# Rows of the right-hand table as one fp32 value or as three bf16 parts, in the edge loop of a graph attention kernel

## The reference

```python
xl = (x @ W_l).reshape(N, HEADS, HEAD_DIM)
xr = (x @ W_r).reshape(N, HEADS, HEAD_DIM)
e = xl[src] + xr[dst]
e = jnp.where(e >= 0, e, NEG_SLOPE * e)
score = jnp.einsum('ehd,hd->eh', e, att)
m = jax.ops.segment_max(score, dst, num_segments=N)
...
ex = jnp.exp(score - m[dst])
denom = jax.ops.segment_sum(ex, dst, num_segments=N)
alpha = ex / (denom[dst] + SM_EPS)
agg = jax.ops.segment_sum(alpha[:, :, None] * xl[src], dst, num_segments=N)
```

## Time and profile before

| | us |
|---|---|
| median of the runs | 1655.17 |
| lowest and highest | 1635.84 and 1659.02 |
| the profiled execution | 1631.12 |
| its span in the profile | 1629.4 |

### The profile page before, as it was taken

The page is one execution under the profiler, slowest core; times in us unless marked ns, Lnnn a source line. Parts: engine busy times, 40 slices in busy tenths (PEclk is TensorE's granted clock), DMA queues, the critical chain, the costliest instruction groups (busy, mean ns, idle before and its releaser), DMA issues. The chain is left out here.

```text
span 1629.4 us, 25059 instructions
## 1 busy us (share of the span) xinstructions
PE 1216.3 (75%) x5659; PEld 863.3 (53%) x5659; DVE 1080.2 (66%) x2307; ACT 846.6 (52%) x3252; POOL 817.7 (50%) x849
## 2 busy tenths in 40 slices
PE   7938677777677777777776768777777756399995
PEld 5426555555455555555554556555555545255663
DVE  7735777677667766776676766786677859313444
ACT  3501366665567557665765676676666813132221
POOL 5454356565456545555555565555656064402223
PEclk9978899989798978999998888999889977599998
DMA  6554357566556655565665666666765125325340
GB/s 184 172 150 114 107 156 172 155 170 163 153 141 169 166 153 143 166 170 157 168 162 138 166 161 167 171 171 166 207 160 137 44 63 178 141 95 151 103 122 17
DMA packets 169375, 238.14 MB, mean 146 GB/s; under 512 B 41666, under 2 KB 135571, under 8 KB 169284
## 3 DMA queue, kind: packets, MB, share of 16 engines
q1 hardware_dynamic: 125188, 130.89, 28.5%
q0 software_dynamic: 41216, 103.67, 24.9%
q10 hardware_dynamic: 2880, 2.66, 0.5%
HBM read 189.57 MB, written 49.58 MB: 147 GB/s over the span
## 5 line engine op out<-in xcount | busy, mean ns | idle before, releaser
L1083 POOL DMA_INDIRECT gathered_rows<-d_xl,e_idx x576 | 547.3, 950 | 420.0 <-ACT e_prod L1512 195.7
L1512 ACT ACTIVATE e_prod<-gathered_rows,e_prod 128x64 f32<-128x64 f32 x2728 | 676.6, 335 | 30.7 <-issue 22.8
L1457 PE MATMUL bank<-e_prod,e_selt 128*128 128x260 f32 x1408 | 409.8, 436 | 157.2 <-DMA gathered_rows<-in_src_dram,n_row_of 68.8
L1457 PEld LDWEIGHTS bank<-e_prod,e_selt 128*128 128x128 f32 x1408 | 286.9, 212 | 250.0 <-issue 89.2
L1403 PE MATMUL bank<-e_xr,e_sel 128*128 128x256 bf16 x2112 | 325.5, 292 | 52.8 <-issue 31.3
L1157 DVE TENSOR_TENSOR e_edge<-bank,gathered_rows 128x512 f32<-128x512 f32 x176 | 119.9, 681 | 285.9 <-remote 271.3
L1403 PEld LDWEIGHTS bank<-e_xr,e_sel 128*128 128x128 bf16 x2112 | 217.6, 105 | 152.6 <-issue 70.1
L1408 PE MATMUL bank<-gathered_rows,ident 128*128 128x256 f32 x704 | 229.4, 406 | 14.0 <-issue 14.0
L1174 DVE TENSOR_REDUCE e_score<-e_edge 128x16 f32<-128x1024 f32 x176 | 213.2, 1211 | 0.3
L1508 ACT ACTIVATE e_prod<-e_diff 128x16 f32<-128x16 f32 x176 | 39.4, 224 | 237.6 <-remote 111.1
L1083 POOL DMA_INDIRECT gathered_rows<-d_xl,src_cols x112 | 106.3, 949 | 105.0 <-issue 29.4
(11 more groups left out here) (315 smaller groups left out, 1105.7 us busy)
## 6 DMA issues: line engine op xcount, KB each, us to landing
e_xr<-d_xr SPq DMA_DIRECT2D x176, 192.0 KB
d_hist<-e_acc SPq DMA_DIRECT2D x176, 130.0 KB
e_drow<-d_rel SPq DMA_DIRECT2D x176, 128.0 KB
w_rows<-in_L_ffn_w_dram SPq DMA_DIRECT2D x16, 1024.0 KB, 7.3
gathered_rows<-d_xl,e_idx POOLq DMA_INDIRECT x576
d_in<-lambda_w SPq DMA_DIRECT2D x18, 387.0 KB
e_rows<-d_rows SPq DMA_DIRECT2D x88, 48.1 KB
x_rows<-in_x_dram SPq DMA_DIRECT2D x8, 512.0 KB, 4.8
```

What stands on the lines that cost most here:

```text
L1083: pool.indirect_dma_start(xl[:, q.slot * G + g, :], None, m.d_xl, bass.IndirectOffsetOnAxis(ap=column, axis=0)).then_inc(gathered[q.slot], 16)
L1457: last = pe.matmul(ps_agg[b], selt[:, b, g, :], flat(prod[:, b, g, :, :]), start=(g == 0), stop=(g == G - 1))
L1512: last = act.activation(prod[:, b, g, h, 0:HEAD], xl[:, q.slot * G + g, h * HEAD:h * HEAD + HEAD], ACT.Copy, scale=prod[:, b, g, h, HEAD:H ...
```

## The change

The right rows are stored once, as fp32. `d_xr` has 256 fp32 columns, a row block is 128 KB, and the survey's steps for the second and third part go (L486, L490, L870); L866 writes the row. The one-hot `sel` becomes fp32. `edges` makes one fp32 one-hot product a group (four a quad in place of twelve), and one fp32 identity product of 512 columns over the adjacent slots of groups 0 and 1 in place of two of 256. The identity product now opens the bank, and the one-hot products of groups 0 and 1 are added to it. The wait for the gathers stands behind groups 2 and 3.

```diff
@@ tensors of the module
-    m.d_xr = dram("d_xr", (PAD, ROW3), BF16)
+    m.d_xr = dram("d_xr", (PAD, DIM))
-    m.xr = sb("e_xr", [P, 4, ROW3], BF16)
+    m.xr = sb("e_xr", [P, 4, DIM])
@@ survey
-    rest = sb("a_rest", [P, 2, DIM])
-    xr3 = sb("a_xr3", [P, RIGHTS, ROW3], BF16)
+    xr1 = sb("a_xr", [P, RIGHTS, DIM])
-                sp.dma_start(m.d_xr[n * P:n * P + P, :], xr3[:, n % RIGHTS, :]).then_inc(stored_r[n % RIGHTS], 16)
+                sp.dma_start(m.d_xr[n * P:n * P + P, :], xr1[:, n % RIGHTS, :]).then_inc(stored_r[n % RIGHTS], 16)
-            def remainder(n):
-                dve.wait_ge(s["hi"], n + 1)
-                if n >= 2:
-                    dve.wait_ge(s["xr"], n - 1)
-                dve.tensor_tensor(rest[:, n % 2, :], ps_rk[n % 4][:, 0:DIM], xr3[:, n % RIGHTS, 0:DIM], ALU.subtract).then_inc(s["rest"], 1)
-
-            def last_part(n):
-                dve.wait_ge(s["mid"], n + 1)
-                dve.tensor_tensor(xr3[:, n % RIGHTS, 2 * DIM:3 * DIM], rest[:, n % 2, :], xr3[:, n % RIGHTS, DIM:2 * DIM],
-                                  ALU.subtract).then_inc(s["xr"], 1)
...
             for n in range(TILES):
-                remainder(n)
                 if n >= 1:
-                    last_part(n - 1)
                     peak(n - 1)
...
-            last_part(TILES - 1)
             peak(TILES - 1)
...
                 if n >= 4:
-                    pe.wait_ge(s["rest"], n - 3)
+                    pe.wait_ge(s["xr"], n - 3)
                     pe.wait_ge(s["keys"], n - 3)
...
-                act.copy(xr3[:, n % RIGHTS, 0:DIM], ps_rk[n % 4][:, 0:DIM]).then_inc(s["hi"], 1)
-
-            def middle_part(n):
-                act.wait_ge(s["rest"], n + 1)
-                act.copy(xr3[:, n % RIGHTS, DIM:2 * DIM], rest[:, n % 2, :]).then_inc(s["mid"], 1)
+                act.copy(xr1[:, n % RIGHTS, :], ps_rk[n % 4][:, 0:DIM]).then_inc(s["xr"], 1)
@@ attend
-    sel = sb("e_sel", [P, 2, QUAD_EDGES], BF16)
+    sel = sb("e_sel", [P, 2, QUAD_EDGES])
...
-                for g in (2, 3, 0, 1):
-                    out = ps_edge[b][g // 2][:, g % 2 * DIM:g % 2 * DIM + DIM]
-                    for part in range(3):
-                        last = pe.matmul(out, sel[:, b, g * P:g * P + P], xr[:, r, part * DIM:part * DIM + DIM],
-                                         start=(part == 0), stop=(part == 2 and g >= 2))
-                    if g < 2:
-                        if g == 0:
-                            pe.wait_ge(gathered[q.slot], (q.turn + 1) * 64)
-                        last = pe.matmul(out, m.ident[:, :], xl[:, q.slot * G + g, 0:DIM], start=False, stop=True)
+                for g in (2, 3):
+                    out = ps_edge[b][1][:, g % 2 * DIM:g % 2 * DIM + DIM]
+                    pe.matmul(out, sel[:, b, g * P:g * P + P], xr[:, r, :], start=True, stop=True)
+                pe.wait_ge(gathered[q.slot], (q.turn + 1) * 64)
+                pe.matmul(ps_edge[b][0][:, :], m.ident[:, :], xl[:, q.slot * G:q.slot * G + 2, 0:DIM], start=True, stop=False)
+                for g in range(2):
+                    out = ps_edge[b][0][:, g * DIM:g * DIM + DIM]
+                    last = pe.matmul(out, sel[:, b, g * P:g * P + P], xr[:, r, :], start=False, stop=(g == 1))
                 last.then_inc(s["edges"], 1)
```

More of the change, by code:

```diff
@@ L44 @@
 ROW = DIM + HEADS
-ROW3 = 3 * DIM
 HCOLS = HEAD + 1
@@ L237, in survey @@
                 "wa scaled norm fixed endsps passed walkps places shifts gathered fetched links shiftps turned turnps taken linksps tables stored linked "
-                "xtps xt right left hi keys rest mid xr xl peak base pair maxps peaks top topps bottom")
+                "xtps xt right left keys xr xl peak base pair maxps peaks top topps bottom")
     FOURS = TILES // 4
@@ L888, in _ @@
                 right_part(n)
-                if n >= 1:
-                    middle_part(n - 1)
-            middle_part(TILES - 1)
 WEIGH_LAG = RUN + 3
```

## The result

The changed kernel takes 1624.1 us (median of 11 runs, 1614.01 to 1632.89), the kernel before in the same series 1652.14 (11 runs). The ratio is 0.985, with a 95% interval of 0.981 to 0.989: 28 us less by the medians. Medians are of all executions, while ratios and intervals leave out those over 1.5% above the fastest of their kernel, so the two can differ by 0.2%.

What follows compares the result with a forecast made beforehand. VectorE's own work was taken to set the pace of `attend`, plus stalls of 271 us. Terms of 10 + 11 - 5 - 1 = +15 us on the median of 1655 gave 1670 us, range 1625 to 1712.

Steps and rivals of the forecast that it cites:

- PE's instruction count: PE's records of `edges` fall from 16 to 10 a quad; of at most 17 us gained, a third counted: -5 us.
- rival B: In `attend`, fewer PE records and 64 KB less a quad take away a fifth of 271 us: 1616 us; chance 0.15.
- nothing in my sum moves it: Test: VectorE's "remote" waits ahead of L1157 stay near 271 us; a move of over 40 us makes the prediction wrong.
- The one-hot on VectorE: L1149 writes fp32 and goes from 356 ns to L2057's 420: +0.064 us a quad, +11 us over 176 quads.
- Rival C: The one-hot falls to the pace of L1157, 0.68 us: 57 us in place of 11, 1716 us; chance 0.05.
- One-hot products on PE: PE's products in `edges`: 2.18 to 2.59 us a quad warm, +0.9 cold; 84 us in all, +10 on the path.
- 13% cold quads: L1403's mean of 0.292 us lies 13% of the way from warm 0.27 to cold 0.42: 23 of 176 quads cold.
- the cold groups: Quads behind the stalls, where PE is slower than VectorE: half of 23 x 0.9 us on the path, +10 us.
- Rival A: PE becomes the bound and paces all quads of the loop outside the stalls: 1720 us; chance 0.20.
- POOL beside the one-hot: The longer one-hot costs an overlapping gather issue on POOL perhaps 0.06 us more, covered by waits for ScalarE: 0.
- Loads: SP's row blocks of 128 KB, not 192, are issued four quads ahead and no wait names them: 0.
- Survey: Three of VectorE's last five operations ahead of the barrier go: -1 us, with 0 and 1.3 as bounds.

## Why the prediction was wrong

**The step that failed** is "PE's instruction count", with its "I count a third: -5 us" and its most of 17. It priced the records by PE's own idle time ahead of L1403 and L1408 (45 us). That was the wrong row: in a stall PE also makes VectorE wait, and that time stands in VectorE's 271 us, under "remote". Adding six records back cost 31 to 37 us (0.019 within one series; 0.0226 against the ratio of another), so a record a quad is worth about 5 to 6 us there. This is shown by adding records. Taking them away was tried with stalls only as two, together with the order (7 to 12 us), so that all six, taken away, give the gain is inferred. I had even read the pace ("PE does 11 matmuls in 18 us") and set an instruction's price of 1.6 us beside it, and then capped the gain by another row.

The mechanism was rival B, "the stalls shrink", which got 15% and the right reason ("in a stall the engines want instructions") beside a wrong one (64 KB less, worth nothing in two runs). That its 1616 us lie near the measured 1624 is luck: it took a fifth of the 271 us away and let the time follow, while two thirds went and the time fell by 28 us.

The rest of the sum with stalls closes only roughly: 31 to 37 us gained by the records and 28 in all leave 3 to 9 for the dearer one-hot and PE's longer products. The 153 us of PE (0.87 a quad) cost some 12 us, two records' price included, so little of the 3 to 9 us can be PE's, and most of VectorE's 24 us doesn't show either. That the stalls' idle time hides it is argued, not shown: no run changed VectorE's work alone with stalls.

**The sentence "nothing in my sum moves it"** on the total of the "remote" waits was the test, and it failed as it should: 271 to 86 us, 56 on the second chip. As a test it is weaker than it looks, though: two records and 0.87 us of PE moved the same total by 88 us, and the time by 12 (18 between the two profiled executions).

**The one-hot on VectorE** was mis-sized: forecast 420 ns and +11 us, measured 495 ns, +139 ns and +24 us of VectorE's time. The row taken, L2057, has four bytes on both sides and 98 partitions, and the new form was not in the trace. The Trainium skill, "VectorE: DVE Perf Modes", section "The perf-mode tier table", gave the estimate of 133 ns, which the trace bears out within 6 ns; I had set it aside for the row. Rival C (680 ns) is out.

**One-hot products on PE:** +0.41 us a quad at full clock, right (2.59 us). The 84 us in all were too many: PE's busy time in the loop rose by 38 (901.60 to 939.31). The step from L1403's mean to 13% cold quads fails as well. By its own numbers it is 15% (0.022 of 0.15 us), or 26 quads, and it takes every longer record for a cold one, while the single records of a stall last 0.37 us too. That the cold groups cost 10 us no run shows. That PE's time is hidden: right with stalls, by the run with 0.87 us more. Rival A, PE as the bound, doesn't come to pass by the change on either kind of chip, but VectorE's 69 us of new waits for PE show it near, and without stalls 0.87 us more a quad is enough for it.

**POOL beside the one-hot:** taken at 0 and small, though not nothing. The issue of a gather takes 958 ns in the mean where it took 950, but one that starts within a one-hot takes 1.04 us in the mean (57 of them; 35 before, 0.97), and the longest of these 1.23 where it was 1.05. The Trainium skill, "SBUF — State Buffer", section "SBUF: two separate sides", has VectorE lock GpSimd out for the whole of such an operation; the trace agrees in kind, with 0.1 us in the mean and 0.3 at most, and as it concerns 57 issues, with about 5 us of POOL, which is idle for 410 us ahead of the same gathers.

**Loads:** 0, right (0.9993 and 0.9998 with the loads cut alone). **Survey:** about -1 us, right: `attend` begins at 92.3 and not 93.1.

Where there are no stalls the forecast's direction holds: 1.0053, 7 us. In the profiles the loop has 931 us against 917 in the run with the order alone (whose time is that of before), VectorE's busy time 879 against 859, its idle time 52 against 58. That it comes near the sum's terms for VectorE and the survey (11 - 1 = 10) is in part luck, since the one-hot cost more than twice its 11 us, and what gave the rest back no run shows. Where the sum fails is the stalls, which cost a fifth of the time on the other chips (1645 against 1332 us).

## What to carry to other kernels

Where a trace has stretches in which the instructions of several engines start at one slow beat, price an edit by the instructions of those engines there and by durations elsewhere, and look for the one with the most instructions a unit of work. A wait without a releaser on one engine can be the price of another engine's instruction count, but its total is no measure of the time lost (174 us at 0.992 of before, 86 at 0.985). And a result of 1 to 2% should be taken on more than one chip: here its sign hangs on it.

## What the runs showed of the hardware that I had not expected

One program, the kernel before, has medians of 1640 to 1652 us in three series and of 1332 to 1333 in three others, two of them on one chip. What separates them in the traces is the stalls: the changed kernel's VectorE idles 311 us of the loop on the one kind and 52 on the other, where the granted clock is also higher, 0.98 against 0.91. The beat of 0.7 us sets in around POOL's rows of gathers on the one kind, and on the other ScalarE's multiplications never show it, though the same gathers take as much of POOL (673 us in a loop of 931). What makes the beat, no run showed, nor whether it belongs to the chip or to what runs beside it.

A compare with bf16 in and fp32 out of 512 columns takes 495 ns, bf16 to bf16 356, fp32 to int32 on 98 partitions 420.
